# An attention layer with precise products: maxima from one-term scores, softmax sums taken after the exponentials, and a new order of the work

## Chip, cores and metric

The kernel runs on one core of one Trainium2 chip. The metric is the device time of one execution in microseconds (us). Engines are named as in the profile: PE (TensorE, matmuls), DVE (VectorE), ACT (ScalarE), POOL (GpSimd), SP (SyncE, here the queue that issues all transfers).

## What is computed

```python
h = _layernorm(x)                                   # x: 16 x 512 x 512
mod = jax.nn.silu(time) @ mod_w + mod_b
shift, scale, gate = jnp.split(mod, 3, axis=-1)
h = h * (scale + 1.0) + shift
qkv = (h @ w_qkv).reshape(B, T, 3, H, e)...         # 16 heads of 32
q = _apply_rope(_layernorm(q, q_norm_w), position)
k = _apply_rope(_layernorm(k, k_norm_w), position)
scores = jnp.einsum('bhqe,bhke->bhqk', q, k) / jnp.sqrt(e)
attn = jax.nn.softmax(scores, axis=-1)
o = jnp.einsum('bhqk,bhke->bhqe', attn, v)
return x + o @ w_out * gate
```

All is float32. The kernel gets its precision from splitting an operand into a rounded high part (type fp32r) and a low part (the rest), and adding three products of parts, "terms": high x high, high x low, low x high.

## The kernel before, in words

**Tiles and groups.** Each of the 16 batches has 512 rows, four tiles of 128: 64 tiles. The 16 heads of a batch make four groups of four heads: 64 groups. In step `s` (0 to 63) the attention of group `s` is done, and beside it the projections of tile `s + 6` (and later the output product of tile `s - 4`). A step has four quarters, one for each 128 rows. `FIRST` to -1 are the steps of the lead-in, without attention.

**A tile.** DVE takes the statistics (L605, L611), the inverse roots by eleven small instructions (`inverse_roots`, L633 to L642) and normalises (L650, L653). PE transposes the tile (`transpose_x`, L252), ACT writes the high part (`x_high`), DVE the low part (`x_low`, L665). PE makes q, k and v (`project`, L261, twelve matmuls each, into bank `Y`). ACT squares and moves q and k (L492, L493) and moves v (L504). DVE sums the squares (L616) and scales (`normalize_qk`, L660), and POOL rotates (`rotate`, L851, L856, L859, for q and for k).

**A group.** PE transposes q and k into the one bank `O` (`transpose_qk`, L352); DVE writes their parts (`qk_parts`, L674, L676). PE then makes the scores twice. By query (`scores_by_query`, L370, three terms of four matmuls in the four banks of `SM` and `MB`): DVE takes the row maxima (`maxima`, L683), ACT the exponentials with their row sums (`query_exponentials`, L527), ACT and DVE the shift `max + log(sum)` (`logarithm`, `log_sum_parts`, L690 to L696), which PE transposes (`transpose_c`, L379). By key (`scores_by_key`, L397, three terms, and L401, which adds the shift by a matmul against ones): ACT takes the exponentials, which are then final probabilities (`key_exponentials`, L542, L543), and PE weighs the values (`weigh_values`, L415, into `O`).

**Output.** ACT moves `O` (L519), DVE splits it (`output_parts`, L712, L714), PE multiplies with `w_out` (`project_out`, L268), DVE applies the gate (L705), POOL adds the residual (L864).

**Order.** Every engine runs its instructions in the order in which they are written, and waits are counts of semaphores. In quarter `q` of step `s`, PE does `scores_by_query(s + 1, q)`, a `weigh_values`, eight matmuls of a projection, `scores_by_key(s, q)` and the last four of the projection. `scores_by_key` waits for the exponentials by query in the same banks (L388).

Of the kernel before, what the change touches and what calls it, by code (L numbers as in the profile page):

```python
# [10 lines left out]
I32 = mybir.dt.int32  # L11

P = 128
RSQRT_MAGIC = 0x5F3759DF
NEWTON = 11


def cond_attention_kernel(nc, x, cond, position, mod_w, mod_b, w_qkv, w_out, q_norm_w, k_norm_w, out):
# [17 lines left out]
    FIRST = -8  # L36
# [12 lines left out]
    def early(s):  # L49
        return s < -1  # L50

    def v_tile(s):
        if s == -1:
            return -1
        return s + 6 if early(s) else s + 5

    with ExitStack() as ctx:
# [3 lines left out]
        def sem(name):  # L61
# [13 lines left out]
        xin = sb("xin", [P, 3, D])  # L75
# [6 lines left out]
        qk_hi = sb("qk_hi", [P, 3, 2, T], F32R)  # L82
        qk_lo = sb("qk_lo", [P, 3, 2, T], F32R)
        cst = sb("cst", [P, TT, P], F32R)
        cT = sb("cT", [P, T], F32R)
        probs = sb("probs", [P, 2, HG, T])
# [5 lines left out]
        negmax = sb("negmax", [P, 2, TT, HG])  # L92
        sums = sb("sums", [P, 2, TT, HG])
        lns = sb("lns", [P, TT, HG])
        row_shift = sb("row_shift", [P, TT, HG])
        bn = sb("bn", [P, 6])
# [3 lines left out]
        newton = sb("newton", [P, 1 + 2 * H])  # L100

# [7 lines left out]
        ld_modw, ld_modb, ld_wout = sem("ld_modw"), sem("ld_modb"), sem("ld_wout")  # L109
        ld_w = [sem("ld_wq"), sem("ld_wk"), sem("ld_wv")]  # L110
        ld_cond, ld_tables = sem("ld_cond"), sem("ld_tables")
        ld_x = [sem("ld_x0"), sem("ld_x1"), sem("ld_x2")]
        ld_res, st_y = sem("ld_res"), sem("st_y")
        ld_gate, ld_ss, ld_last, st_mod = sem("ld_gate"), sem("ld_ss"), sem("ld_last"), sem("st_mod")
# [3 lines left out]
        qkT_done, qm_done, cT_done, s_done, pv_step = (  # L118
            sem("qkT_done"), sem("qm_done"), sem("cT_done"), sem("s_done"), sem("pv_step"))
        siluT_done, mod_product = sem("siluT_done"), sem("mod_product")  # L120

        h_hi, squared, raw_out, v_out, o_out = (
            sem("h_hi"), sem("squared"), sem("raw_out"), sem("v_out"), sem("o_out"))
        qm_exp, ln_done, cT_out, s_exp = sem("qm_exp"), sem("ln_done"), sem("cT_out"), sem("s_exp")
        cond_exp, w_high, mod_out, wout_high = sem("cond_exp"), sem("w_high"), sem("mod_out"), sem("wout_high")
# [3 lines left out]
        x_scaled, h_lo, qk_high, qk_low, max_out, c_step, c_ready, y_gated = (  # L129
            sem("x_scaled"), sem("h_lo"), sem("qk_high"), sem("qk_low"), sem("max_out"), sem("c_step"),  # L130
            sem("c_ready"), sem("y_gated"))
        o_high, o_low, last_high, last_low, wout_low = (
            sem("o_high"), sem("o_low"), sem("last_high"), sem("last_low"), sem("wout_low"))
        ident_ready, silu_step, silu_ready, siluT_ready = (
            sem("ident_ready"), sem("silu_step"), sem("silu_ready"), sem("siluT_ready"))
        w_step, w_centred, w_low, table_step, tables_ready, stats_set, last_added = (
            sem("w_step"), sem("w_centred"), sem("w_low"), sem("table_step"), sem("tables_ready"),
            sem("stats_set"), sem("last_added"))

        consts, rope_step, res_added = sem("consts"), sem("rope_step"), sem("res_added")  # L140
# [3 lines left out]
        modw_raw = rows[:].rearrange("p a t j d -> p (a t j d)")[:, 4 * D:4 * D + DT * 3 * D].rearrange(  # L144
            "p (c n) -> p c n", c=DT)
        cond_sb = oT[0:NB, 0, 0, :]
        silu_sb = oT[0:NB, 0, 1, :]
        siluT = oT[:, 0, 2, 0:DT * NB].rearrange("p (c b) -> p c b", c=DT)
# [26 lines left out]
        def _(sp):  # L175
# [7 lines left out]
            for t in range(2):  # L183
                sp.dma_start(xin[:, t, :], x_t[0, t]).then_inc(ld_x[t], 16)
# [6 lines left out]
            def load_x(n):  # L191
                sp.wait_ge(xT_done, n - 2)
                sp.dma_start(xin[:, n % 3, :], x_t[n // TT, n % TT]).then_inc(ld_x[n % 3], 16)
# [704 lines left out]
```

## Time and profile before

| | |
|---|---|
| median of 3 runs | 1943.38 us (1943.3 to 1945.53) |
| profiled execution | 1946.49 us, span 1944.7 us |
| busy, share of the span | PE 91%, ACT 76%, DVE 76%, POOL 22% |
| lead-in, to the first `transpose_c` | 142.0 us |
| a step in the middle | 27.9 us |
| the last five steps | 160 us |

The table is read so: the middle, 59 steps, is 85% of the span. In it PE does nearly all the time something, while each other engine has gaps; ahead of it and behind it PE has gaps.

### The profile page before, as it was taken

What the parts mean: (1) busy time and instruction counts of PE and PEld (TensorE: products, weight loads), DVE (VectorE), ACT (ScalarE), POOL (GpSimd) and SP (SyncE); (2) the same over time, 40 slices, a digit from 0 to 9 for tenths busy, and PEclk for the clock granted to TensorE, in tenths of its full rate; (3) what the DMA queues carried; (4) which work ended last, traced back from release to release, by engine and by line L of the source; (5) the groups of instructions that cost most, each with busy time, mean ns of one, the idle gap of its engine ahead of it and who ended that gap; (6) DMA issues with size and microseconds to landing.
All of it is one profiled execution on the core that took longest, in us unless ns stands there. A gap on an engine that the chain in (4) does not pass through costs nothing.

```text
span 1944.7 us, 35999 instructions
## 1 busy us (share of the span) xinstructions
PE 1776.7 (91%) x13346; PEld 1030.4 (53%) x13346; DVE 1485.0 (76%) x2430; ACT 1487.2 (76%) x3145; POOL 434.4 (22%) x452
## 2 busy tenths in 40 slices
PE   4768899999999999999999999999999999997777
PEld 1645555555555555555555555555555555554333
DVE  6677778888888788878887888788878888875443
ACT  2248888888888888888888888888888888887663
POOL 0331222122212221222122212221222122221000
PEclk8879999999999999999999999999999999998769
DMA  5000010100101111010101010010111002000001
GB/s 193 27 6 28 6 44 23 50 28 17 55 28 50 34 39 34 23 55 17 55 28 50 23 49 29 18 55 28 50 33 40 28 17 63 16 28 22 21 18 66
DMA packets 35950, 72.77 MB, mean 37 GB/s; under 512 B 4513, under 2 KB 4513, under 8 KB 35778
## 3 DMA queue, kind: packets, MB, share of 16 engines
q1 hardware_dynamic: 35778, 70.47, 11.3%
q8 instruction: 109, 1.79, 0.4%
q14 instruction: 63, 0.52, 0.1%
HBM read 53.58 MB, written 16.88 MB: 36 GB/s over the span
## 4 chain that ended last, share of the span: by engine, by line
PE 80%; ACT 9%; issue 5%; DVE 5%; DMA 1%; ACTq 0%; SPq 0%; DVEq 0%
PE Y L261 26%; PE SM L370 13%; PE SA L397 10%; PE O L415 10%; PE Y L268 10%; ACT SM L527 4%; PE SA L401 3%; PE O L352 3%; PE SA L252 2%; ACT vals L504 2%; PE SA L379 2%; DVE qk_lo L676 1%; DVE qk_hi L674 1%; ACT probs L542 1%; ACT oT L519 1%
## 5 line engine op out<-in xcount | busy, mean ns | idle before, releaser
L527 ACT ACTIVATE SM<-SM,negmax 128x512 f32<-128x512 f32 x512 | 338.7, 664 | 130.8 <-DVE negmax L683 130.8
L683 DVE TENSOR_REDUCE negmax<-SM 128x2 f32<-128x1024 f32 x256 | 313.6, 1225 | 162.6 <-PE MB L370 155.9
L851 POOL TENSOR_TENSOR pair_part<-rows,rope_pair 128x256 f32<-128x256 f32 x128 | 94.5, 739 | 1312.8 <-DVE rows L660 1307.7
L527 ACT ACTIVATE MB<-MB,negmax 128x512 f32<-128x512 f32 x512 | 341.9, 671 | 0.0
L542 ACT ACTIVATE probs<-SM 128x1024 f32<-128x1024 f32 x256 | 262.8, 1027 | 72.0 <-PE SM L401 54.6
L683 DVE TENSOR_REDUCE negmax<-MB 128x2 f32<-128x1024 f32 x256 | 310.9, 1215 | 0.0
L261 PE MATMUL Y<-wqkv_hi,hT_hi 128*128 128x512 f32 x728 | 307.4, 422 | 0.3 <-ACT rows L493 0.3
L261 PE MATMUL Y<-wqkv_hi,hT_lo 128*128 128x512 f32 x728 | 306.7, 421 | 0.0
L415 PE MATMUL O<-probs,vals 128*32 128x512 f32 x2048 | 283.8, 627 | 5.9 <-ACT probs L543 5.9
L261 PE MATMUL Y<-wqkv_lo,hT_hi 128*128 128x512 f32 x728 | 289.2, 397 | 0.0
L543 ACT ACTIVATE probs<-SA 128x1024 f32<-128x1024 f32 x256 | 260.8, 1019 | 0.0
L261 PEld LDWEIGHTS Y<-wqkv_hi,hT_hi 128*128 128x128 f32 x728 | 139.1, 191 | 116.4 <-ACT rows L493 98.0
L674 DVE CAST qk_hi<-O 128x512 fp32r<-128x512 f32 x128 | 88.6, 692 | 146.0 <-PE O L352 146.0
L261 PEld LDWEIGHTS Y<-wqkv_hi,hT_lo 128*128 128x128 f32 x728 | 138.8, 191 | 67.6 <-issue 42.6
L370 PE MATMUL SM<-qk_hi 32*128 32x512 f32 x512 | 131.8, 499 | 45.2 <-ACT probs L542 18.6
L856 POOL TENSOR_TENSOR rows<-rows,rope_same 128x512 f32<-128x512 f32 x128 | 164.8, 1287 | 10.0
L397 PE MATMUL SA<-qk_hi 32*128 32x512 f32 x512 | 128.8, 496 | 38.5 <-ACT SM L527 37.8
L261 PEld LDWEIGHTS Y<-wqkv_lo,hT_hi 128*128 128x128 f32 x728 | 139.2, 191 | 24.3
L370 PEld LDWEIGHTS SM<-qk_hi 32*128 32x128 f32 x512 | 54.3, 187 | 147.9 <-issue 140.1
L370 PE MATMUL MB<-qk_hi 32*128 32x512 f32 x512 | 131.6, 510 | 0.0
L397 PE MATMUL SM<-qk_hi 32*128 32x512 f32 x512 | 129.9, 502 | 0.0
L510 ACT ACTIVATE cT<-SA 128x512 fp32r<-128x512 f32 x64 | 38.4, 600 | 109.9 <-PE SA L379 109.9
(140 smaller groups left out, 4108.6 us busy)
## 6 DMA issues: line engine op xcount, KB each, us to landing
xin<-in_x_dram SPq DMA_DIRECT2D x64, 256.0 KB, 2.9
xres<-in_x_dram SPq DMA_DIRECT2D x60, 256.0 KB, 2.6
out_dram<-xres SPq DMA_DIRECT2D x60, 256.0 KB, 2.0
shift_scale<-mod_rows SPq DMA_DIRECT2D x16, 512.0 KB, 4.2
gate<-mod_rows SPq DMA_DIRECT2D x16, 256.0 KB, 4.7
rows<-in_L_cond_mod_w_dram SPq DMA_DIRECT2D x1, 3072.0 KB, 10.0
probs<-in_L_cond_w_qkv_dram SPq DMA_DIRECT2D x2, 1024.0 KB, 12.7
vals<-in_L_cond_w_qkv_dram SPq DMA_DIRECT2D x1, 1024.0 KB, 15.6
```

What stands on the lines that cost most here:

```text
L261: mm = pe.matmul(bank, a[:, k, :], w[:, k, j * D:(j + 1) * D], start=(m == 0), stop=(m == 11))
L268: mm = pe.matmul(bank, o[:, g, :], w[:, g, :], start=(m == 0), stop=(m == 11))
L370: mm = pe.matmul(qm_bank(i), a[r, ring, 0, cols], c[r, ring, 1, :], start=(a is qk_hi and c is qk_hi), stop=(a is qk_lo))
L397: pe.matmul(s_bank(i), a[r, ring, 1, cols], c[r, ring, 0, :], start=(a is qk_hi and c is qk_hi), stop=False)
L415: mm = pe.matmul(O[head_rows(i), :], vals[:, b % 2, t, E * h:E * (h + 1)], probs[:, n % 2, i, :], start=(t == 0), stop=(t == TT - 1), skip ...
L527: ins = act.activation(qm_bank(i), qm_bank(i), ACT.Exp, bias=negmax[:, g % 2, t, i:i + 1], accum_out=sums[:, g % 2, t, i:i + 1])
L542: act.activation(probs[:, n % 2, 2:4, :], SM[:], ACT.Exp).then_inc(s_exp, 1)
L543: act.activation(probs[:, n % 2, 0:2, :], SA[:], ACT.Exp).then_inc(s_exp, 1)
L674: dve.tensor_copy(qk_hi[:, i, j, :], O[:]).then_inc(qk_high, 1)
L683: dve.tensor_reduce(negmax[:, g % 2, t, 2 * half:2 * half + 2], bank[:], AX.X, ALU.max, negate=True).then_inc(max_out, 1)
L851: pool.tensor_tensor(pair_part[:].rearrange("p h (i two) -> p h i two", two=2), swapped, rope_pair[:, t, j, :].rearrange("p (i two) -> p i ...
L856: pool.tensor_tensor(r, r, rope_same[:, t, j, :].unsqueeze(1).to_broadcast([P, H, E]), ALU.mult).then_inc(rope_step, 1)
```

## The change

- `scores_by_query` makes only the first term, high x high: four matmuls in place of twelve. From it come the maxima alone. `query_exponentials`, `logarithm` and `log_sum_parts` are gone; DVE writes the negated maxima straight into `cst`.
- The exponentials by key are thus not yet divided by their sum. The four probability blocks of a group (128 keys x 4 heads x 512 queries each, three buffers) are added: block 1 onto block 0 by POOL, block 2 by a transfer that POOL issues and that adds at its destination, block 3 by POOL (`add_keys`). PE sums over the 128 keys with ones (`add_over_keys`, into `MB`), ACT makes the inverse (`log_sums`, `inverse_sums`), DVE multiplies it onto the output (`scale_o`). The last group has two PE sums in place of the third addition.
- q and k are transposed into `MB`, both at once; ACT writes their high parts (`high_qk`), DVE the low parts (`low_qk`). Two buffers in place of three.
- `inverse_roots` has four instructions in place of eleven, and starts from a guess that ACT makes with Ln and Exp (`guess_roots`). ACT squares from `rows` behind the move.
- Step and quarters are reordered: a projection is twelve matmuls in one piece, v of tile `s + 4`, q and k of tile `s + 6`, the output product of tile `s - 5`. `output_parts` stands first in a step on DVE.
- The lead-in is written out by hand: weights in another order, modulation in three pieces (four matmuls at once in four column blocks, then one matmul that adds the blocks), its first row straight into `shift_scale`. POOL makes two of the low parts of the weights. Rotations wait for the third modulation piece (`mod_partial`).

```diff
+    def sum_buffer(g):
+        return 2 * (g % 2)
+    def probs_buffer(g, t):
+        return 1 if t % 2 else (sum_buffer(g) if t == 0 else 2 - sum_buffer(g))
...
             def scores_by_query(g, t):
...
+                if t == 1 and g >= 2:
+                    pe.wait_ge(sum_ln, g - 1)
                 if n > 0:
-                    pe.wait_ge(qm_exp, 2 * n)
...
+                    pe.wait_ge(max_out, 2 * n)
+                if g > 0:
+                    pe.wait_ge(s_exp, 2 * (n - TT) + 1)
...
-                for a, c in ((qk_hi, qk_hi), (qk_hi, qk_lo), (qk_lo, qk_hi)):
-                    for i in range(HG):
...
+                for i in range(HG):
+                    r = head_rows(i)
+                    mm = pe.matmul(qm_bank(i), qk_hi[r, g % 2, 0, cols], qk_hi[r, g % 2, 1, :], start=True, stop=True)
...
             def transpose_c(g):
-                pe.wait_ge(c_ready, g + 1)
+                pe.wait_ge(max_out, 2 * TT * (g + 1))
...
-                pe.wait_ge(qm_exp, 2 * (n + TT) + 1 if group(g + 1) else 2 * TT * NS)
...
+                if group(g + 1) or t == 0:
+                    pe.wait_ge(max_out, 2 * (n + TT - 1) + 1)
...
+            def add_over_keys(g, bank, buffers):
...
+                        mm = pe.matmul(bank[head_rows(i), :], ones_r[:, 0:E].bitcast(F32), probs[:, a, i, :],
...
+            modulation_parts(1, SM[:, 1, :])
+            modulation_parts(0, SM[:, 0, :])
...
+            project(3, 2, MB[:, 1, :])
+            modulation_parts(2, O[:])
...
+                    pe.wait_ge(third_added, s)
...
+                    add_over_keys(s - 1, MB[:, 0, :], (sum_buffer(s - 1),))
...
+            def high_qk(g, j):
+                act.wait_ge(qkT_done, 2 * g + j + 1)
...
+                act.activation(sum_inv[:], bank, ACT.Ln).then_inc(sum_ln, 1)
...
+                act.activation(sum_inv[:], sum_inv[:], ACT.Exp, scale=-1.0).then_inc(sum_ready, 1)
...
+                            act.wait_ge(second_added, 16 * g)
...
+                        act.wait_ge(third_added, g)
...
+                        act.wait_ge(first_added, g + 1)
...
-                for i in (2 * half, 2 * half + 1):
-                    ins = act.activation(qm_bank(i), qm_bank(i), ACT.Exp, bias=negmax[:, g % 2, t, i:i + 1],
-                                         accum_out=sums[:, g % 2, t, i:i + 1])
...
+            def scale_o(g):
+                o = oT[:, (g // NG) % 2, g % NG, :]
+                dve.wait_ge(sum_ready, g + 1)
+                dve.wait_ge(o_out, g + 1)
+                dve.tensor_tensor(o, o, sum_inv[:], ALU.mult).then_inc(o_scaled, 1)
...
+            def add_keys(g, t):
+                to = probs[:, sum_buffer(g)].rearrange("p h n -> p (h n)")
+                more = probs[:, probs_buffer(g, t)].rearrange("p h n -> p (h n)")
+                pool.wait_ge(s_exp, 2 * (TT * g + t) + 2)
+                if t == 1:
+                    pool.wait_ge(pv_step, TT * g + 1)
+                    pool.tensor_tensor(to, to, more, ALU.add).then_inc(first_added, 1)
+                elif t == 2:
+                    pool.wait_ge(first_added, g + 1)
+                    pool.dma_start(to, more, accum_op=ALU.add).then_inc(second_added, 16)
+                else:
+                    pool.wait_ge(second_added, 16 * (g + 1))
+                    pool.tensor_tensor(to, to, more, ALU.add).then_inc(third_added, 1)
...
+            pool.wait_ge(mod_partial, 3)
+            for n in range(5):
+                rotate(n, 0)
+                rotate(n, 1)
```

The order on POOL, a step in the middle. Before, a tile's rotation (L851, L856, L859, for q and for k) and a residual (L864):

```order
L864 TENSOR_TENSOR xres<-xres,gated 128x512
L851 TENSOR_TENSOR pair_part<-rows,rope_pair 128x256
L856 TENSOR_TENSOR rows<-rows,rope_same 128x512
L859 TENSOR_TENSOR rows<-rows,pair_part 128x16x16
L851 TENSOR_TENSOR pair_part<-rows,rope_pair 128x256
L856 TENSOR_TENSOR rows<-rows,rope_same 128x512
L859 TENSOR_TENSOR rows<-rows,pair_part 128x16x16
```

And in the changed kernel (L1176 and L1182 are the additions of block 1 and block 3, L1179 the adding transfer):

```order
L1176 TENSOR_TENSOR probs<-probs 128x2048
L1179 DMA probs<-probs 128x2048
L1153 TENSOR_TENSOR pair_part<-rows,rope_pair 128x256
L1158 TENSOR_TENSOR rows<-rows,rope_same 128x512
L1161 TENSOR_TENSOR rows<-rows,pair_part 128x16x16
L1153 TENSOR_TENSOR pair_part<-rows,rope_pair 128x256
L1158 TENSOR_TENSOR rows<-rows,rope_same 128x512
L1161 TENSOR_TENSOR rows<-rows,pair_part 128x16x16
L1182 TENSOR_TENSOR probs<-probs 128x2048
L1166 TENSOR_TENSOR xres<-xres,gated 128x512
```

Three instructions were added, and the rotation now stands between the issue of the transfer and the addition that waits for it.

The order on DVE around the start of a step. Before, from the maxima of the last quarter (`negmax`) to the split of the output:

```order
L683 TENSOR_REDUCE negmax<-SM 128x2
L683 TENSOR_REDUCE negmax<-MB 128x2
L674 CAST qk_hi<-O 128x512
L676 TENSOR_TENSOR qk_lo<-O,qk_hi 128x512
L674 CAST qk_hi<-O 128x512
L676 TENSOR_TENSOR qk_lo<-O,qk_hi 128x512
L683 TENSOR_REDUCE negmax<-SM 128x2
L683 TENSOR_REDUCE negmax<-MB 128x2
L616 TENSOR_REDUCE stats<-squares 128x16
L605 BN_STATS bn<-xin 128x6
L712 CAST o_hi<-oT 128x512
L714 TENSOR_TENSOR o_lo<-oT,o_hi 128x512
```

And now (L938 maxima, L960 and L962 the split of the output):

```order
L945 TENSOR_TENSOR oT<-oT,sum_inv 128x512
L905 SCALAR_TENSOR_TENSOR xin<-xin,stats,shift_scale 128x512
L908 SCALAR_TENSOR_TENSOR xin<-xin,rstd,shift_scale 128x512
L860 BN_STATS bn<-xin 128x6
L866 BN_AGGR stats<-bn 128x2
L938 TENSOR_REDUCE cst<-SM 128x2
L938 TENSOR_REDUCE cst<-MB 128x2
L872 TENSOR_REDUCE stats<-squares 128x16
L960 CAST o_hi<-oT 128x512
L962 TENSOR_TENSOR o_lo<-oT,o_hi 128x512
L927 TENSOR_TENSOR qk_lo<-MB,qk_hi 128x512 x2
```

The split of the output moved ahead of the low parts of q and k, and three instructions with two operands in SBUF (L945, L905, L908) stand ahead of the last maxima.

## Rows read from the trace of the kernel before

**Rows 1.** Windows by stage: time, each engine busy (x instructions), granted clock, DMA share

```profile
100.00:142.00 42.00, 24.05 (x133) 16.55 (x131) 32.22 (x56) 17.19 (x44) 13.66 (x14) 0.77 0.01 2
170.00:1785.00 1615.00, 1547.48 (x12020) 900.79 (x12012) 1303.32 (x2115) 1332.92 (x2837) 389.74 (x402) 1.00 0.11 34
1785.00:1907.00 122.00, 91.80 (x651) 43.61 (x649) 54.58 (x69) 80.38 (x172) 4.53 (x4) 0.71 0.07 20
```

**Rows 2.** Timeline of PE: start us, us, operation; the end of a quarter

```profile
932.82 0.50 PE L261 MATMUL Y<-wqkv_hi,hT_lo 128*128 128x512 f32 x1
933.16 0.40 PE L261 MATMUL Y<-wqkv_hi,hT_hi 128*128 128x512 f32 x1
933.39 0.39 PE L261 MATMUL Y<-wqkv_lo,hT_hi 128*128 128x512 f32 x1
...
934.12 0.49 PE L370 MATMUL SM<-qk_hi 32*128 32x512 f32 x2
...
935.03 1.06 PE L415 MATMUL O<-probs,vals 128*32 128x512 f32 x8
936.02 0.50 PE L261 MATMUL Y<-wqkv_hi,hT_hi 128*128 128x512 f32 x1
```

**Rows 3.** Timeline of PE, `transpose_c` of two early steps, without output product

```profile
198.76 0.54 PE L379 MATMUL SA<-ident_r,cst 128*128 128x128 f32 x4
```

```profile
226.00 0.54 PE L379 MATMUL SA<-ident_r,cst 128*128 128x128 f32 x4
```

**Rows 4.** Chain in the middle, start us, us, what: two `transpose_c` in a row

```profile
921.83 0.47 PE SA L379 x4
...
949.72 0.47 PE SA L379 x4
```

**Rows 5.** Groups of instructions: count, busy us, mean ns, idle before

```profile
L527 ACT ACTIVATE SM<-SM,negmax 128x512 f32<-128x512 f32 x512 | 338.7, 664 | 130.8 <-DVE negmax L683 130.8
L683 DVE TENSOR_REDUCE negmax<-SM 128x2 f32<-128x1024 f32 x256 | 313.6, 1225 | 162.6 <-PE MB L370 155.9
```

**Rows 6.** Timelines of DVE and POOL at one moment: who holds up whom

```profile
945.67 0.74 POOL L851 TENSOR_TENSOR pair_part<-rows,rope_pair 128x256 f32<-128x256 f32 x1 [20.66 <-DVE rows L660]
946.49 1.29 POOL L856 TENSOR_TENSOR rows<-rows,rope_same 128x512 f32<-128x512 f32 x1
...
951.61 1.27 POOL L864 TENSOR_TENSOR xres<-xres,gated 128x512 f32<-128x512 f32 x1
```

```profile
946.55 1.27 DVE L694 CAST cst<-row_shift 128x16 fp32r<-128x16 f32 x1
...
947.96 0.69 DVE L705 TENSOR_TENSOR gated<-Y,gate 128x512 f32<-128x512 f32 x1
```

**Rows 7.** The same cast with POOL idle, and a POOL add beside a long DVE subtract

```profile
1842.21 0.18 DVE L694 CAST cst<-row_shift 128x16 fp32r<-128x16 f32 x1
```

```profile
100.52 2.30 DVE L790 TENSOR_TENSOR wout_lo<-oT,wout_hi 128x2048 fp32r<-128x2048 f32 x1 [1.12 <-ACT wout_hi L567]
```

```profile
100.75 2.67 POOL L859 TENSOR_TENSOR rows<-rows,pair_part 128x256 f32<-128x256 f32 x1
```

**Rows 8.** DMA issues: KB each, median us from issue to landing

```profile
xin<-in_x_dram SPq DMA_DIRECT2D x64, 256.0 KB, 2.9
...
rows<-in_L_cond_mod_w_dram SPq DMA_DIRECT2D x1, 3072.0 KB, 10.0
...
vals<-in_L_cond_w_qkv_dram SPq DMA_DIRECT2D x1, 1024.0 KB, 15.6
oT<-in_L_cond_w_out_dram SPq DMA_DIRECT2D x1, 1024.0 KB, 12.0
```

**Rows 9.** Chain of the last steps, one quarter: start us, us, what

```profile
1789.12 1.03 ACT probs L542
...
1791.99 1.24 DVE negmax L683
...
1796.97 1.03 ACT probs L542
```

More of the change, by code:

```diff
@@ L231, in _ @@
                     load_residual(s - 4)
+                if tile(s + 8) and (s + 8) % TT == 0:
+                    load_shift_scale((s + 8) // TT)
+            store(NT - 5)
             sp.wait_ge(qkT_done, 2 * NS)
@@ L464, in _ @@
+            pe.wait_ge(last_low, 3)
+            for t in range(3):
+                project_last(t, 2, 3)
+            weigh_values(LAST, 3)
+            pe.wait_ge(second_added, 16 * NS)
+            add_over_keys(LAST, SM[:, 0, :], (sum_buffer(LAST), probs_buffer(LAST, 3)))
+            project_last(3, 0, 3)
             pe.wait_ge(last_low, NG)
             for t in range(TT):
-                project_last(t, last_banks[t], 3, 4)
+                project_last(t, 3, 4)
         @block.scalar
@@ L585, in _ @@
+            log_sums(LAST, SM[:, 0, :])
+            inverse_sums(LAST)
         @block.vector
@@ new lines, in _ @@
+            x_statistics(6)
+            aggregate_x(6)
+            low_qk(0, 0)
+            low_qk(0, 1)
+            square_sums(4, 1)
+            maxima(0, 0)
+            x_low(5)
+            inverse_roots(6)
+            maxima(0, 1)
+            normalize_qk(4)
+            maxima(0, 2)
+            normalize_x(6)
+            maxima(0, 3)
+            x_statistics(7)
+            aggregate_x(7)
+            square_sums(5, 0)
+            for s in range(LAST + 1):
+                if s - 5 >= 0:
+                    output_parts(s - 5)
+                if group(s + 1):
+                    low_qk(s + 1, 0)
+                    low_qk(s + 1, 1)
+                    maxima(s + 1, 0)
+                if tile(s + 5):
+                    square_sums(s + 5, 1)
+                if group(s + 1):
+                    maxima(s + 1, 1)
+                if tile(s + 6):
+                    x_low(s + 6)
+                if s - 5 >= 0:
+                    apply_gate(s - 5, Y[:], gated[:])
+                if tile(s + 5):
+                    inverse_roots(s + 7)
+                    normalize_qk(s + 5)
+                if group(s + 1):
+                    maxima(s + 1, 2)
+                if s == LAST:
+                    output_parts(s - 4)
+                if s > 0:
+                    scale_o(s - 1)
+                if s == 1:
+                    dve.wait_ge(wout_high, 1)
+                    dve.tensor_tensor(wout_lo[:], wout_raw, wout_hi[:].bitcast(F32), ALU.subtract
+                                      ).then_inc(wout_low, 1)
+                if tile(s + 7):
+                    normalize_x(s + 7)
+                if tile(s + 8):
+                    x_statistics(s + 8)
+                    aggregate_x(s + 8)
+                if group(s + 1):
+                    maxima(s + 1, 3)
+                if tile(s + 6):
+                    square_sums(s + 6, 0)
+                if s == LAST:
+                    last_parts(0)
+                    last_parts(1)
+                    last_parts(2)
+                    apply_gate(s - 4, Y[:], gated[:])
```

1023 lines of the change are left out of this document (600 added, 423 removed).

## The prediction

> **What bounds the kernel now.** I read the windows by stage first. In the middle PE is busy 1547.5 of 1615 us at full granted clock, ACT and DVE some 1300 to 1330, POOL 390 [rows 1]. So PE is the first bound there, with the others close. The two ends are not at PE's bound: in the 42 us ahead of the first `transpose_c` PE is busy 24, and in the last steps 92 of 122 at a granted clock of 0.71. Then the timeline of PE, by starts, since matmuls overlap: a full matmul follows the last after 0.23 us, the first after a switch of shape after 0.34; three terms by query take from 934.12 to 935.03, 0.91 us; a `weigh_values` 0.99 [rows 2]. A step in the middle is 27.9 us from one `transpose_c` to the next [rows 4]. Early steps, which have no output product (3 us of PE), still take 27.24 us [rows 3]: PE is not alone, the loop of maxima and exponentials by query is as long. Both must shrink for a gain, and both do here.
>
> **The floor of the new step on PE.** Per step, by starts: four `scores_by_key` of 1.13 are 4.5; five sums over keys and values (four `weigh_values`, one `add_over_keys` of the same shape) of 0.99 are 5.0; four `scores_by_query` of one term, 0.91 less two terms of 0.23, are 1.8; three projections of twelve in one piece, 0.34 + 11 x 0.23 + 0.1 for leaving, are 8.9; the output product 3.0; transposes 1.9. Sum 25.1. Before, the same count gives 27.0 and the step 27.9. So PE's own work falls by 1.9 and another 0.9 of waits can go.
>
> **The other engines.** ACT loses sixteen exponentials by query, 0.66 us each [rows 5], 10.6 a step, and gains some six moves and small ones of 0.5 to 0.6, so it has much slack. DVE loses two casts, seven small ones and the shift, and gains `scale_o`; before it is busy 1303 us in 57.9 steps [rows 1], 22.5 a step, now by count 19 to 20, of it four pairs of maxima at some 2.3 [rows 5]. POOL gains two additions of 128x2048. From 0.74 us for 256 and 1.29 for 512 elements [rows 6], 2.15 ns an element, one is 4.6 us. POOL then has 9.3 + 5.9 (rotation) + 1.3 (residual) + the issue of the transfer, which no row shows; I take 1 us, between 0.3 and 2. That is 17.6, under 25.
>
> **By hand through one step**, zero at `transpose_c(s)`. Scores by key end at 2.5, first exponentials at 3.6, `low_qk` can end at 3.2, so `scores_by_query` starts at 3.7 (0.2 of wait). v to 7.1; key scores; `add_over_keys` at 8.2, which needs the third addition of the group before; output product and transpose to 14.25; then two quarters of 5.8 with 0.2 wait each for the SM half of the exponentials. End 25.8. The maxima of the last quarter would be done before `transpose_c` by 0.4. So waits that are in sight cost 0.7: **25.8**.
>
> **What POOL's long instructions do to DVE.** The trace shows the price. A cast of 16 elements takes 0.18 us with POOL idle and 1.27 beside a POOL multiplication that ends at 947.78; DVE's gate product, which reads PSUM, runs beside POOL at its 0.69 [rows 6, 7]. The other way round, POOL's add of 0.74 took 2.67 beside a DVE subtract of two SBUF operands and ended 0.6 after it [rows 7]. So the one that comes later stands still until the other's instruction ends. The page SBUF — State Buffer of the Trainium skill, section Who interferes with whom, says this of a DVE instruction with two SBUF inputs or a two-port mode against one of GpSimd that reads SBUF; by that rule, the trace agrees.
> Where do they meet in the new order? (a) Inverse roots at 15.1 against the first addition, 11.0 to 15.6: 0.5, hidden. (b) `scale_o` and the two normalisations, from 20.0, against the rotation, from 18.5 (exponentials of quarter 2 end at 17.5, issue 1 us). Each can wait for a rest of 0.6 to 1.3. With all three waits the last maxima end 1.7 late, and `transpose_c` with them; with none, 0. I take half, 0.8: a step of **26.6**. (c) The split of the output at about 0.6 to 1.7 of the step, against the third addition. That depends on when the addition starts, so on the transfer.
>
> **The transfer.** 1 MB within SBUF with addition is in no row. Between 256 KB in 2.9 us and 3072 KB in 10.0 [rows 8] 1 MB takes 4.8; since it reads both operands, 7.3 if reads count double. The row of the same size, 1024 KB of 128 x 2048, took 12.0, behind other loads. I take 11, nearest to the row of that size; the ends are 4.8 and 15.6, the longest landing of a load of that size [rows 8]. Issued at 17.5 it lands at 28.5, 1.9 into the next step: the split of the output is past, the exponentials of quarter 0 wait for it only from 2.6, and the third addition ends at 6.5, before 8.2. Then it costs nothing. The page DMA: Bandwidth & Descriptors of the Trainium skill, section Anatomy of one DMA, gives a fixed 2 us and bytes / 436e3 for a transfer issued by GpSimd, an estimate of 4.4 us here; by it the third addition starts as soon as the rotation ends, and the time would be that of the first rival below. No run here shows it yet.
>
> **Lead-in.** Before: 142.0, where the window of rows 1 ends. The modulation came first, then its round trip through memory, then each tile in one chain with eleven small instructions. Now: 3 MB of weights have landed at about 12, by 10.0 for 3072 KB [rows 8]; modulation pieces and the two additions to about 20, normalisation, first projection at about 24, twelve projections of 3.0 (some at half clock) to about 63. Rotations wait for the third modulation piece, so they run from 64, and group 0 needs four of 5.9 [rows 6]: 88. Then three projections, four maxima: first `transpose_c` at **107**, between 92 and 125.
>
> **Tail.** A quarter was 7.85 [rows 9]: exponentials, scores, maxima, exponentials by query, scores. Without the exponentials by query it is about 5.2 at half clock and 4.2 at full. With the output product and the sum in one quarter a step of 19 to 29; I take 23 in place of 30.5 (122 us for four, [rows 1]). The last step was some 37, from 1907 to the end at 1944.7; it loses exponentials but gains the wait for the last transfer, two sums, Ln, Exp and the scaling: 43.
>
> **Sum.** 107 + 5 early steps of 25.7 (128.5) + 53 steps of 26.6 (1410) + 2 with v alone of 22 (44) + 3 x 23 (69) + 43 = 1801.5 of span. Before, 1.8 us lie outside the span, and the median is 3.1 under the profiled run: **1800**. Against 1943.4 that is 7.4% less: 35 from the lead-in, 75 from the middle, the rest from the tail and the steps with no q and k.
>
> **Rivals.**
> *The split of the output is caught by the third addition; slower.* If the transfer lands within about 9 us, the third addition starts when the rotation ends, about 1 before the next step, and holds the port to 3.6. The cast stands until then, the residual add may slip in between cast and subtract (1.3), `low_qk` comes at 5 to 6 in place of 1.9, and `scores_by_query`, with the projection queued behind it on PE, starts 2.3 to 3.6 late. A step is 29.5 to 30.8, the whole 53 x 3.0 to 53 x 4.2 more: 1960 to 2025. It becomes slower than before from a step of 29.3. For it: the interpolated 4.8 to 7.3. Against it: no row shows a POOL instruction of over 1.3 us holding DVE, and with a landing like that of the 1024 KB loads, 12.0 or more, the addition comes after the split. Chance 0.13.
> *No meeting costs anything.* DVE's instructions fall in gaps, the step is 25.8 or a little under, the lead-in 95: 1745. Chance 0.22.
> *The transfer is late*, 13 to 15.6: quarter 0's exponentials wait, each us over 11.7 costs one a step, 58 in all: 1870 to 1980. Chance 0.13, a third of it slower than before.
> *The forecast's own case*, 1765 to 1850, chance 0.50. Two hundredths are left for surprises of the tail.
>
> **How the numbers follow.** The range of 8 in 10 takes the forecast's case, most of the case without meetings and the better half of the late transfer: 1735 to 1915. About 0.2% is what a measurement of this kernel can tell from no change. Faster: 0.50 + 0.22 + 0.08 + 0.02 + 0.01 of the first rival = 0.83; same 0.02; slower 0.15.
>
> **What would show it.** The distance between two `transpose_c` in the middle: 26.6, with PE waiting for the last maxima by under 1.7. In DVE's timeline the cast of the split at its 0.41 and not at 3 to 5; on POOL two adds of 4.6 a step; the landing of the adding transfer 10 to 12 after issue; the first `transpose_c` near 107. The prediction is wrong if the cast stretches, if exponentials of quarter 0 wait for the transfer, or if PE's granted clock in the middle is under 1.00.

## The result and the profile after

The changed kernel takes 2079.49 us (2070.99 to 2087.37, 4 runs) where the kernel before took 1943.34 beside it: the ratio is 1.0697, interval 1.0643 to 1.0752. It is slower by 7%, where 7.4% faster was forecast. Its profiled execution, the slowest of the four, took 2087.37, with a span of 2085.6. The forecast made the span up from six stages, of which the two steps with v alone and the three behind them are taken together here as the tail; measured by the starts of the copy of `cT` (L647), which follows each `transpose_c`, they are:

| stage | forecast us | measured us | miss us |
|---|---|---|---|
| lead-in, to the first `transpose_c` | 107 | 115.6 | +8.6 |
| 5 early steps | 128.5 | 142.2 | +13.7 |
| 53 steps | 1410 (26.6 each) | 1650.5 (31.1 each, median 30.8) | +240.5 |
| 5 steps of the tail | 113 | 134.0 | +21.0 |
| last step | 43 | 43.2 | +0.2 |

So 240 of the 284 us lie in the middle. The page of the changed kernel, against [rows 1, 5, 8]: busy time of the engines, the chain that ended last by engine and by line, three groups (busy us and mean ns of one after the bar, then idle before), and the new transfer's landing.

```profile
PE 1739.2 (83%) x11822; PEld 1030.8 (49%) x11822; DVE 1588.6 (76%) x1714; ACT 959.8 (46%) x1420; POOL 1143.7 (55%) x648
...
DVE 42%; PE 42%; issue 13%; ACT 1%; POOL 1%; DMA 1%; SPq 0%; DVEq 0%; POOLq 0%; ACTq 0%
...
L1176 POOL TENSOR_TENSOR probs<-probs 128x2048 f32<-128x2048 f32 x64 | 294.4, 4601 | 658.1 <-ACT probs L706 648.5
...
L1182 POOL TENSOR_TENSOR probs<-probs 128x2048 f32<-128x2048 f32 x63 | 287.5, 4564 | 38.6 <-DMA probs<-probs 38.6
...
L960 DVE CAST o_hi<-oT 128x512 fp32r<-128x512 f32 x60 | 199.5, 3325 | 0.0
...
probs<-probs POOLq DMA_DIRECT2D x64, 1024.0 KB, 7.0
```

More than half of the chain is not PE's. The line to stop at is L960: a cast of 128x512, which takes 0.42 us where nothing is in its way (below), has a mean of 3325 ns. The additions took the 4.6 us that were worked out for them, and the transfer landed after 7.0 on the median (6.9 to 9.2), not 11. Windows of the middle of the changed kernel (columns as in rows 1), which answer to the second row of [rows 1]:

```profile
258.00:1910.00 1652.00, 1417.10 (x9775) 846.19 (x9773) 1312.68 (x1373) 784.95 (x1169) 948.12 (x530) 0.94 0.27 65
```

PE is busy 86% of the stretch, in place of 96%, and its granted clock is 0.94 in place of 1.00. One step shows why. Timelines of POOL, of DVE and of PE, from one `transpose_c` (1000.46) on; the next step follows after 30.86:

```profile
998.58 0.74 POOL L1161 TENSOR_TENSOR rows<-rows,pair_part 128x256 f32<-128x256 f32 x1
999.28 4.56 POOL L1182 TENSOR_TENSOR probs<-probs 128x2048 f32<-128x2048 f32 x1
1003.80 1.44 POOL L1166 TENSOR_TENSOR xres<-xres,gated 128x512 f32<-128x512 f32 x1
```

```profile
1000.91 3.21 DVE L960 CAST o_hi<-oT 128x512 fp32r<-128x512 f32 x1
1004.16 1.64 DVE L962 TENSOR_TENSOR o_lo<-oT,o_hi 128x512 fp32r<-128x512 f32 x1
1005.72 1.28 DVE L927 TENSOR_TENSOR qk_lo<-MB,qk_hi 128x512 fp32r<-128x512 f32 x2
```

```profile
1000.46 0.54 PE L370 MATMUL SA<-ident_r,cst 128*128 128x128 f32 x4 [0.74 <-DVE cst L938]
...
1002.96 1.06 PE L411 MATMUL O<-probs,vals 128*32 128x512 f32 x8
1007.05 0.50 PE L362 MATMUL SM<-qk_hi 32*128 32x512 f32 x2 [3.03 <-DVE qk_lo L927]
...
1007.49 1.42 PE L308 MATMUL Y<-wqkv_hi,hT_hi 128*128 128x512 f32 x4
1008.71 1.91 PE L311 MATMUL Y<-wqkv_hi,hT_lo 128*128 128x512 f32 x4
1010.41 1.68 PE L315 MATMUL Y<-wqkv_lo,hT_hi 128*128 128x512 f32 x4
```

The third addition of the sums (block 3, by POOL) starts as the last rotation ends, 1.2 ahead of `transpose_c`, and ends at 1003.84. The cast stands from 1000.91 to 1004.12. POOL's residual addition then runs beside the subtract, which takes 1.64. The low parts of q and k come at 5.3 to 6.5 of the step, and PE, which has nothing else in its order, waits 3.03. Then it runs the projection of v, twelve matmuls, in 4.5 us instead of 3.0. The windows of those pieces give the clock:

```profile
1000.46:1007.40 6.94, 3.90 (x40) 2.25 (x40) 6.50 (x5) 4.52 (x7) 4.79 (x2) 1.00 0.10 38
1007.40:1012.02 4.62, 4.62 (x16) 3.31 (x12) 2.95 (x3) 0.00 (x0) 0.00 (x0) 0.63 0.49 170
1012.02:1031.32 19.30, 18.14 (x133) 10.42 (x132) 15.14 (x19) 10.27 (x15) 13.12 (x9) 1.00 0.32 69
```

After the stall the granted clock is 0.63, a mean over a piece spent mostly at 1.2 GHz; before and behind it is 2.4. So a step is the floor of 25.1, plus 3.0 of stall, 1.5 of clock, 0.7 of waiting for the last maxima (the first row of PE above) and 0.5 of the small waits by hand: 30.8.

In 13 of the 53 steps the transfer landed later than the rotation ended, and the addition started 0.7 to 1.5 later than in the others. That made it worse, not better: the cast was held for 4.0 to 4.7 us in place of 3.2, and those steps took 31.6 to 33.7.

### The profile page after: what moved, and what is told of

It reads as the page before. It is cut to its first block, busy times and chain, and to the rows that moved or that the text cites. A ratio compares the mean times of both kernels' runs of the same rounds, so it can differ in the third digit from the quotient of the medians.

```text
span 2085.6 us, 31004 instructions
## 1 busy us (share of the span) xinstructions
PE 1739.2 (83%) x11822; PEld 1030.8 (49%) x11822; DVE 1588.6 (76%) x1714; ACT 959.8 (46%) x1420; POOL 1143.7 (55%) x648
## 4 chain that ended last, share of the span: by engine, by line
DVE 42%; PE 42%; issue 13%; ACT 1%; POOL 1%; DMA 1%; SPq 0%; DVEq 0%; POOLq 0%; ACTq 0%
DVE cst L938 11%; DVE o_hi L960 9%; PE Y L321 8%; PE Y L308 6%; PE Y L311 5%; PE SA L392 4%; PE Y L315 4%; PE SM L362 4%; DVE oT L945 3%; DVE qk_lo L927 3%; PE O L411 3%; DVE xin L905 3%; PE MB L420 3%; DVE half_var L884 3%; DVE rows L915 2%
## 5 line engine op out<-in xcount | busy, mean ns | idle before, releaser
L1176 POOL TENSOR_TENSOR probs<-probs 128x2048 f32<-128x2048 f32 x64 | 294.4, 4601 | 658.1 <-ACT probs L706 648.5
L938 DVE TENSOR_REDUCE cst<-SM 128x2 fp32r<-128x1024 f32 x256 | 311.8, 1218 | 382.7 <-PE MB L362 382.7
L362 PE MATMUL SM<-qk_hi 32*128 32x512 f32 x512 | 139.6, 534 | 210.6 <-DVE qk_lo L927 177.2
L938 DVE TENSOR_REDUCE cst<-MB 128x2 fp32r<-128x1024 f32 x256 | 311.5, 1217 | 0.0
L1182 POOL TENSOR_TENSOR probs<-probs 128x2048 f32<-128x2048 f32 x63 | 287.5, 4564 | 38.6 <-DMA probs<-probs 38.6
L308 PE MATMUL Y<-wqkv_hi,hT_hi 128*128 128x512 f32 x724 | 254.6, 480 | 1.7 <-ACT hT_hi L590 1.7
L311 PE MATMUL Y<-wqkv_hi,hT_lo 128*128 128x512 f32 x724 | 229.3, 445 | 2.4 <-DVE hT_lo L921 2.4
L621 ACT ACTIVATE rows<-Y 128x512 f32<-128x512 f32 x123 | 73.5, 597 | 306.4 <-PE Y L315 306.4
L315 PE MATMUL Y<-wqkv_lo,hT_hi 128*128 128x512 f32 x724 | 211.9, 419 | 0.0
L641 ACT ACTIVATE vals<-Y 128x512 f32<-128x512 f32 x61 | 36.5, 598 | 360.7 <-PE Y L315 360.7
L960 DVE CAST o_hi<-oT 128x512 fp32r<-128x512 f32 x60 | 199.5, 3325 | 0.0
## 6 DMA issues: line engine op xcount, KB each, us to landing
probs<-in_L_cond_w_qkv_dram SPq DMA_DIRECT2D x2, 1024.0 KB, 11.2
```

The lines of the kernel that those rows point to most:

```text
L308: pe.matmul(bank, x_hi[:, k, :], wqkv_hi[:, k, cols], start=(k == 0), stop=False)
L311: pe.matmul(bank, x_lo[:, k, :], wqkv_hi[:, k, cols], start=False, stop=False)
L315: mm = pe.matmul(bank, x_hi[:, k, :], wqkv_lo[:, k, cols], start=False, stop=(k == DT - 1))
L362: mm = pe.matmul(qm_bank(i), qk_hi[r, g % 2, 0, cols], qk_hi[r, g % 2, 1, :], start=True, stop=True)
L938: dve.tensor_reduce(heads[:, 2 * half:2 * half + 2, 0], bank[:], AX.X, ALU.max, negate=True).then_inc(max_out, 1)
L960: dve.tensor_copy(o_hi[:], oT[:, b % 2, :, cols]).then_inc(o_high, 1)
```

## Experiments

Each theory's numbers stand in the expectations. Step means the time from one `cT` copy to the next in the middle, the median where nothing else is said. Experiments 1, 5 and 7 were timed three or four times, the others once. Five runs of the kernel before beside them lie within 0.2% of each other and the four of the changed kernel within 0.8%, so differences of some 50 us are read, and ones of 3 us are not.

### 1. The split of the output behind the first maxima

```
                if group(s + 1):
                    low_qk(s + 1, 0)
                    low_qk(s + 1, 1)
                    maxima(s + 1, 0)
+               if s - 5 >= 0:
+                   output_parts(s - 5)
```

(and the pair of lines that calls `output_parts` ahead of `low_qk` gone). 

> The changed kernel with one edit: DVE's split of the output (cast L960 and subtract L962) stands behind the maxima of quarter 0, not ahead of the low parts of q and k. Port theory (the third addition on POOL holds the split, 2.8 us, the residual add the subtract, 0.95, and PE stands 3.0 us and then runs 1.5 us longer at half clock): the split now falls where POOL idles, cast 0.41 us, the step falls from 30.8 to 26.0 to 27.4 us, the whole to 1830 to 1910. Rival, the load theory (the step is long because DVE, POOL and PE together have too much to do, so that work moved only moves the wait): 30 us or more a step, 2040 to 2090.

Measured: 1824.35 us, ratio to the kernel before 0.9382 (0.9361 to 0.9403); step 26.5. One move of two instructions on DVE turns 7% slower into 6% faster. The middle and, on DVE, the split and `scale_o`:

```profile
258.00:1650.00 1392.00, 1317.02 (x9699) 779.82 (x9697) 1099.83 (x1367) 779.76 (x1161) 931.88 (x524) 1.00 0.31 77
```

```profile
L945 DVE TENSOR_TENSOR oT<-oT,sum_inv 128x512 f32<-128x512 f32 x63 | 82.0, 1301 | 0.0
...
L960 DVE CAST o_hi<-oT 128x512 fp32r<-128x512 f32 x60 | 26.7, 444 | 0.0
```

The cast is back at 444 ns and the clock at 1.00, while all additions and the transfer are still there. A step lost 4.4 us by the meeting (30.84 to 26.45); stall and clock had been counted at 4.5. The step lies in the range of the port theory, the whole 6 us under it.

### 2. The third addition behind the split

```
                     pool.wait_ge(second_added, 16 * (g + 1))
+                    if g >= 4:
+                        pool.wait_ge(o_low, g - 3)
```

> The changed kernel with one more wait on POOL and nothing moved on DVE: the third addition waits for the split of the output of the next step (o_low). Port theory: the addition starts 1.7 us into the step in place of 1.1 ahead of it, ends at 6.3, ahead of the 8.2 at which PE needs it; the step falls to 26.6 to 27.4 as with the late split, the whole to 1850 to 1910. Load theory: a wait more on POOL can only cost, 31 us or more a step.

Measured: 1820.94 us, step 26.4. Here DVE's order is the changed kernel's own, and only POOL is told to wait. The group of the third addition:

```profile
L1184 POOL TENSOR_TENSOR probs<-probs 128x2048 f32<-128x2048 f32 x63 | 289.2, 4591 | 184.7 <-DVE o_lo L962 178.5
```

A wait of 178.5 us in sum on POOL, 2.8 a step, gains 259 us of time. The cause is the moment of the meeting, not DVE's order. The step is 0.2 and the whole 29 under the lower ends of the port theory.

### 3. The additions cut to 16 columns

```
-                    pool.tensor_tensor(to, to, more, ALU.add)
+                    pool.tensor_tensor(to[:, 0:16], to[:, 0:16], more[:, 0:16], ALU.add)
```

(both additions; the sums leave out most columns, and the logarithm gets a small bias.) 

> The changed kernel with POOL's two additions cut to the first 16 of 2048 columns (the softmax sums are then incomplete; the transfer, all waits and all other work stay; the logarithm gets a small bias). It measures what the two additions cost in all. Port theory: with them gone only the rotation and the residual meet DVE: 25.8 to 26.6 us a step, 1800 to 1850. Load theory: POOL's 9.2 us a step were not on the path, since POOL idles a third of the time: 29 us or more a step.

Measured: 1825.31 us, step 26.5. The first addition, and DVE's half variance and `scale_o`, in this kernel:

```profile
L1176 POOL TENSOR_TENSOR probs<-probs 128x16 f32<-128x16 f32 x64 | 14.3, 224 | 688.9 <-ACT probs L706 688.9
```

```profile
L945 DVE TENSOR_TENSOR oT<-oT,sum_inv 128x512 f32<-128x512 f32 x63 | 105.4, 1674 | 0.0
...
L884 DVE TENSOR_SCALAR half_var<-stats 128x33 f32<-128x33 f32 x64 | 11.1, 173 | 0.3
```

With 553 us less work on POOL than in experiment 1 (581.8 us busy against 1134.9) the step is that of experiments 1 and 2. Both numbers are in the port theory's range. So 9 us of additions a step cost nothing but the meeting with the split. (The meeting (a) of the forecast, of the half variance with the first addition, is seen to go: 173 ns against 996 in experiment 1; nothing came of it, as was said.) `scale_o`, which stands beside the rotation, is still held: there is the rest of the loss.

### 4. A transfer that lands late

```
                     pool.dma_start(to, more, accum_op=ALU.add).then_inc(second_added, 16)
+                    pool.dma_start(spare, wqkv_hi[:, :, 0:D]).then_inc(spare_out, 16)
...
                     pool.wait_ge(second_added, 16 * (g + 1))
+                    pool.wait_ge(spare_out, 16 * (g + 1))
```

> The changed kernel with a second transfer of 1 MB (weights to a spare place in memory, used by nothing) issued by POOL behind the adding one, and the third addition waits for both. It gives the third addition the late start that the prediction had assumed (11 us after issue in place of 7.0). Port theory: if both have landed 11 to 13 us after the issue, the split passes ahead of the addition and the step falls to 27 to 28 us, the whole to 1880 to 1940, faster with more transfers. If it costs POOL a second issue of 0.9 us and DVE meets a later rotation, up to 29. Load theory: 31 us or more.

Measured: 1828.33 us, step 26.4. The third addition and the landings of the two transfers:

```profile
L1186 POOL TENSOR_TENSOR probs<-probs 128x2048 f32<-128x2048 f32 x63 | 295.6, 4693 | 161.3 <-DMA spare<-wqkv_hi 157.1
...
probs<-probs POOLq DMA_DIRECT2D x64, 1024.0 KB, 7.1
spare<-wqkv_hi POOLq DMA_DIRECT2D x64, 1024.0 KB, 9.8
```

This is the forecast's case made true: 1 MB of traffic more a step, and the kernel is 251 us faster than the changed one, since the addition starts 0.9 to 2.9 behind `transpose_c` (median 1.6) and no longer 1.2 ahead of it, and the cast, which starts 0.45 behind it, gets past. The experiment's own ranges, 27 to 28 a step and 1880 to 1940 in all, were too high; the forecast of 26.6 a step holds where the transfer is as late as it assumed.

### 5. `scale_o` moved too

The pair ahead of `low_qk` is gone as in experiment 1, and `scale_o` is for the group one step earlier.

```
                     maxima(s + 1, 0)
+                if s > 1:
+                    scale_o(s - 2)
+                if s - 5 >= 0:
+                    output_parts(s - 5)
...
-                if s > 0:
+                if s == LAST:
                     scale_o(s - 1)
```

> Nothing is left out of the computation. Edit on the changed kernel: output_parts(s-5) and scale_o both stand behind maxima(s+1,0) on VectorE, scale_o for the group before the last (s-2), so nothing that reads two SBUF operands stands between the rotation of GpSimd and maxima(s+1,3) but the two normalisations. In the kernel that moved the split alone a step is 26.5, of it 0.7 a wait of the transposition of the maxima for the last maxima. Meeting theory: scale_o stood behind the rotation there; without it the last maxima come at least 0.7 earlier, that wait goes and a step is 25.7 to 26.0: 1780 to 1800 in all. Rival theory: the normalisations hold VectorE as before, and the multiplication, now near the second long addition, only moves the loss: 26.3 to 26.7, 1815 to 1835.

Measured: 1773.02 us (1771.82 to 1775.86), ratio 0.9118 (0.9103 to 0.9133); step 25.5, in all 53 steps. That is 0.2 and some 7 us under the lower ends of the meeting theory. Windows of the middle, and DVE beside POOL's first addition, which runs from 1004.86 to 1009.49:

```profile
258.00:1600.00 1342.00, 1306.50 (x9676) 782.68 (x9676) 1074.37 (x1367) 772.31 (x1158) 914.79 (x525) 1.00 0.33 80
```

```profile
1006.83 0.68 DVE L921 TENSOR_TENSOR hT_lo<-SA,hT_hi 128x512 fp32r<-128x512 f32 x1
1007.95 0.69 DVE L953 TENSOR_TENSOR gated<-Y,gate 128x512 f32<-128x512 f32 x1 [0.44 <-PE Y L321]
1008.56 0.97 DVE L884 TENSOR_SCALAR half_var<-stats 128x33 f32<-128x33 f32 x1
```

```profile
1004.86 4.63 POOL L1178 TENSOR_TENSOR probs<-probs 128x2048 f32<-128x2048 f32 x1 [4.62 <-ACT probs L706]
```

PE is busy 97% of the middle and waits nowhere but 0.2 for the exponentials in three quarters of four: this is the by-hand step without a meeting that costs (25.8), three tenths shorter. The rival, that the loss would only move, falls, though the two normalisations still meet the rotation. The rows also show which of these instructions of DVE ran beside a long addition: the two that read PSUM take their 0.68 and 0.69, while the half variance, which reads and writes SBUF alone, ends when the addition ends.

### 6. The projection of v ahead of the stall

```
                 if tile(s + 4):
                     ...
                     project(s + 4, 2, Y[:])
+                if group(s + 1):
+                    scores_by_query(s + 1, 0)
```

(in the changed kernel, on TensorE; the pair of lines ahead of it gone.) 

> Nothing is left out. Edit on the changed kernel: in quarter 0 on TensorE the projection of v stands ahead of scores_by_query(s+1,0), in place of behind it; VectorE and GpSimd are as in the changed kernel, so the cast is still held 3.2 us. A step is 30.8 there. If the hold costs only because TensorE has nothing to do until the low parts come, the 3.0 of the projection fills the gap at full clock: the stall falls from 3.0 to under 0.5 ahead of the query scores, the 1.5 us that the projection took longer at half clock go too, and a wait for the first maxima of about 1 comes in ahead of scores_by_key(s,1): a step of 27.7 to 28.5, 1900 to 1945 in all, with a granted clock of 0.98 or more in the middle. If the low clock has another cause than the stall, the clock in the middle stays at 0.94 and a step is 29.2 to 30: 1980 to 2030.

Measured: 1957.72 us, mean step 28.6, granted clock 0.98. Most steps take 27.8; 21 of 53 take 29.5 or more, each with a stretch at 1.2 GHz in it, and in 11 steps PE still waits 0.6 to 1.6 for the low parts. The time lies past the upper end of the first theory (28.5 a step, 1945) and well under the other's (29.2, 1980). The waits of PE from 300 to 1500, and the windows of quarter 1 in a long and in a short step (the sum over keys, values and the output product):

```profile
PE SA L392 <- DVE cst L938: 58.5, 41, 1.4
PE SA L370 <- DVE cst L938: 32.5, 42, 0.8
...
PE SM L362 <- DVE qk_lo L927: 8.2, 8, 1.6
```

```profile
1013.42:1021.96 8.54, 8.54 (x53) 4.13 (x53) 4.53 (x5) 4.09 (x7) 3.60 (x1) 0.80 0.11 34
...
1043.00:1049.85 6.85, 6.85 (x56) 3.96 (x56) 4.50 (x5) 4.09 (x7) 3.03 (x1) 1.00 0.15 43
```

The cast is held as long as before (3.2, same order), but the stall of 3.0 is filled; in its place comes a wait of 1.4 for the first maxima. 25.5 + 1.4 + 0.8 for the last maxima is 27.7, which is the short step. So most of the loss comes from PE having nothing to do at that moment, and the low clock goes with the stall in 32 of 53 steps, where the changed kernel had it in every one. In the long steps it comes back, right behind the wait of 1.4: quarter 1 takes 8.54 with PE busy throughout, at a clock of 0.80, where the short step takes 6.85. The wait ahead of it is the same 1.4 in both. Why the clock falls behind one of them and not behind the other stays open.

### 7. The third modulation piece early

```
             project(1, 1, MB[:, 0, :])
+            modulation_parts(2, O[:])
             pe.wait_ge(v_out, 1)
...
             project(3, 2, MB[:, 1, :])
-            modulation_parts(2, O[:])
```

(on the kernel of experiment 5.) 

> Nothing is left out. The kernel with both moves, and the eight matmuls of the third modulation piece on TensorE after project(1,1), near 47 us, in place of after project(3,2), near 64. Theory: in the changed kernel GpSimd idles 32.3 us until that piece, then rotates four tiles back to back until 89.7, and the first cT copy is at 115.6. With the piece early each rotation follows its normalisation (the last at 64.8), so they end near 71 to 73 and the first cT copy comes at 97 to 102: 14 to 18 us less than the same kernel without it, about 1765 to 1785 in all. Rival: rotations beside the normalisations hold VectorE, the projections of the lead-in wait and half is lost: first copy at 104 to 110, 6 to 11 us less.

Measured: 1759.78 us (1758.06 to 1761.23), ratio 0.9047 (0.9033 to 0.9060): the fastest of all. The first `cT` copy is at 102.5 in place of 115.6, between the two expectations. POOL's first rotation in the changed kernel, then the first and the last for group 0 here, and what then took time on PE:

```profile
64.96 1.10 POOL L1153 TENSOR_TENSOR pair_part<-rows,rope_pair 128x256 f32<-128x256 f32 x1 [32.26 <-PE O L435]
```

```profile
47.52 0.74 POOL L1155 TENSOR_TENSOR pair_part<-rows,rope_pair 128x256 f32<-128x256 f32 x1 [14.81 <-DVE rows L915]
...
76.29 0.73 POOL L1163 TENSOR_TENSOR rows<-rows,pair_part 128x256 f32<-128x256 f32 x1
```

```profile
73.30 2.08 PE L311 MATMUL Y<-wqkv_hi,hT_lo 128*128 128x512 f32 x4 [4.37 <-DVE hT_lo L921]
```

The gain of 13 us is 1 short of the theory's 14, and the whole 5 under its 1765. The rotations end at 77.0, not at 71 to 73, since the last normalisation now stands behind small instructions of DVE that rotations hold (0.74, 1.23 and 0.78 us for ones of 0.18 to 0.20), and the projection of tile 4 waits for DVE's queue. The theory is right in the main, 13 us, and the rival's mechanism is seen at work for the rest.

### 8. Three terms by query, with the split late

```
-                for i in range(HG):
+                for a, c in ((qk_hi, qk_hi), (qk_hi, qk_lo), (qk_lo, qk_hi)):
+                    for i in range(HG):
...
```

(on the kernel of experiment 1.) 

> Nothing is left out. The kernel with the split late (1824.35, step 26.5), with scores_by_query in three terms in place of one, as in the kernel before: two terms more cost TensorE 0.46 for each of four tiles, 1.8 a step. If TensorE's own work now bounds the step, it is 28.0 to 28.4 and the whole 1910 to 1940. If VectorE's chain of maxima bounds it, half or less shows: 26.8 to 27.5, 1845 to 1885.

Measured: 1886.28 us, step 27.4, 0.95 over experiment 1. By the expectation's words the step (26.8 to 27.5) speaks for the chain of maxima as the bound (the whole is 1 us over that theory's 1885). Its window says something finer:

```profile
300.00:1700.00 1400.00, 1365.07 (x11045) 823.25 (x11047) 1048.02 (x1328) 750.32 (x1124) 906.37 (x510) 1.00 0.31 75
```

PE is busy 97.5% and no wait for the last maxima is left. 25.5, the step with PE as the bound (experiment 5), plus the 1.84 of two terms in four tiles (0.23 each) is 27.3. So with one term the bound was the chain of the last maxima with `scale_o` held in it, at 26.5, and with three it is PE. By these numbers one term is worth 1.9 a step when the meetings are gone too and 0.95 when they are not; three terms in the order of experiment 5 were not run.

### 9 and 10. What the transfer costs

```
-                    pool.dma_start(to, more, accum_op=ALU.add).then_inc(second_added, 16)
+                    pool.dma_start(to, more).then_inc(second_added, 16)
```

> Edit on the kernel with both moves (1773.02 us): the transfer of 1 MB within SBUF copies in place of adding, so the sums leave out two of four parts (the logarithm gets a bias so that it stays finite). It measures what the addition in the transfer costs. If the price is the bytes moved, operands read twice (the 7.3 of the forecast's working), a copy lands in 4.6 to 5.2 us after its issue in place of 7.0. If the addition is free and the price lies in the packets, it stays at 6.5 to 7.0. The total tells nothing here: GpSimd rotates until after the landing in both, 1768 to 1778.

```
+                    pool.dma_start(to[:, 0:1024], more[:, 0:1024], accum_op=ALU.add).then_inc(second_added, 16)
```

> Edit on the kernel with both moves: the adding transfer takes 1024 of the 2048 columns, 512 KB, so the sums leave out part of one tile (the logarithm gets a bias so that it stays finite). If the price is a fixed part of some 2 us and the rest goes by bytes, it lands in 4.3 to 4.8 us; if it is set by the number of rows and packets and not by bytes, in 6 to 7. The total stays at 1768 to 1778.

The landings, of the copy and of the half, beside 7.0 for the whole addition:

```profile
probs<-probs POOLq DMA_DIRECT2D x64, 1024.0 KB, 4.6
```

```profile
probs<-probs POOLq DMA_DIRECT2D x64, 512.0 KB, 4.5
```

Both are as expected of a price by bytes. From 7.0 and 4.5 an adding transfer costs 2.0 us and 5.0 per MB, if it goes by a fixed part and bytes; if the copy has the same 2.0, it costs 2.6 per MB, and the addition about doubles the part that goes by bytes. The copy was taken at one size only, so its fixed part is assumed. The totals, 1773.37 and 1776.12, are within 3.1 of experiment 5: in that order the landing does not matter. The page DMA: Bandwidth & Descriptors of the Trainium skill, section Anatomy of one DMA, gives 2 us and bytes / 436e3, an estimate of 4.4 for 1 MB; the copy agrees with it at 4.6, the adding transfer, at 7.0, does not.

## Why the prediction was wrong

**The step that failed is the choice of 11 us for the transfer.** With it the third addition was put behind the split of the output, and the meeting (c) at nothing. The forecast had worked out 4.8 from the rows of other sizes, and 7.3 "if reads count double"; then it took 11, "nearest to the row of that size". The chip gave 4.6 for a copy and 7.0 for the adding one: both worked numbers were right within 0.3. The rows of 12.0 and 15.6 [rows 8] are loads of the start, in flight with megabytes of others. Windows of the kernel before while they ran (columns as in rows 1, with GB/s last):

```profile
15.00:20.00 5.00, 5.00 (x10) 0.86 (x9) 3.81 (x14) 0.59 (x1) 0.00 (x0) 1.00 1.05 399
20.00:25.00 5.00, 5.00 (x12) 0.89 (x11) 4.93 (x4) 0.59 (x1) 0.00 (x0) 1.00 1.05 387
```

All sixteen DMA engines are busy the whole time, so these rows hold the delay of other loads and say little of what a transfer costs by itself. Size was the wrong likeness; what else is in flight was the right one.

**A threshold made this step decisive.** The forecast said itself that a landing within about 9 us brings the third addition ahead of the next `transpose_c`, and the first rival priced what follows: a step of 29.5 to 30.8, 1960 to 2025 in all. Measured is 30.8. Up to the stall the mechanism is the rival's to the letter: the addition starts 1.2 ahead of the step (it said 1), holds to 3.4 (3.6), the residual addition slips in between cast and subtract (1.64 for the subtract), the low parts come at 5.3 to 6.5 (5 to 6), PE waits 3.03 (2.3 to 3.6). Its chance of 0.13 was the same error again, since it rested on the price of 11. "No row shows a POOL instruction of over 1.3 us holding DVE" was weak evidence: in the trace of before only one POOL instruction is longer than 1.4 us, the 2.67 of rows 7, and that one was itself held. The page SBUF — State Buffer of the Trainium skill, section Who interferes with whom, gives the shared ports to whichever instruction comes first, for the whole of it. By that rule, the trace agrees: the cast took 3.2 us, until the 4.56 of the addition were over.

**What the rival left out.** It reached 30.8 with a start of the projection up to 3.6 late and 0.6 more that it does not account for; measured are 3.0 of stall and 1.5 of low clock behind it, which is in no term. That its 30.8 is met is in part luck. That a stall costs clock too could be read in [rows 1], where the tail ran at 0.71. The time of 2087 lies past the rival's upper end of 2025: 18 us because the mean step is 31.1 and not 30.8 (the 13 late landings above, 11.2 us of waiting in sum), and 44 at the ends (8.6, 13.7 and 21.0 in the table).

**What held.** PE's floor of 25.1 and the by-hand 25.8: measured 25.5 in experiment 5. The forecast of 26.6 with meeting (b) and without (c): 26.4 to 26.5 in experiments 1, 2 and 4. The price of meeting (b) taken as 0.8: 1.0 between experiments 1 and 5, of it 0.8 as the wait for the last maxima. The additions at 4.6 us (4564 and 4601 ns), the issue at 1 us (0.88), the last step at 43 (43.2). The tail holds in part: without the meeting its five steps take 121.4 and 121.6 in experiments 1 and 5, against 113 forecast, and 134.0 with it. In experiment 1 the last three take 23.7 each on the mean (23 forecast), but the two with v alone take 25.1 each (22 forecast).

**Lead-in and early steps** were taken too short by 22 together in the changed kernel. The rotations ended at 89.7, near the 88 of the forecast, but the four maxima behind them took 26 us rather than 19. The windows of the changed kernel from that moment, and two of PE's waits there:

```profile
90.54:115.62 25.08, 15.69 (x64) 10.38 (x63) 15.47 (x21) 4.47 (x10) 6.27 (x6) 0.77 0.04 11
```

```profile
99.83 1.66 PE L311 MATMUL Y<-wqkv_hi,hT_lo 128*128 128x512 f32 x4 [1.84 <-DVE hT_lo L921]
...
110.71 0.80 PE L362 MATMUL SM<-qk_hi 32*128 32x512 f32 x2 [2.89 <-DVE cst L938]
```

PE and DVE wait for each other in turn, tile by tile, at a clock of 0.77; the estimate had counted instructions and no such turns. The five early steps have the same look: 142.2 at a clock of 0.91 in the changed kernel, still 139.5 in experiment 5, of them 30.7 for the first alone. They have no split of the output, so the meeting with it is not their cause. Which wait sets them was not tried.

By the sum: with the rival's 30.8 a step and the measured ends the span is 2067, 18 short of the measured 2085.6. With the transfer as late as was assumed, 1828.33 (experiment 4) against a forecast of 1800 is a miss of 1.6%: the ends were taken 35 us too short and the middle 10 too long.

Three slips in the working bear on nothing above. The line through the rows of 256 and 3072 KB gives 7.4, not 7.3, with reads counted double. POOL's terms add up to 17.5, not 17.6. By its own rule of one us a step for each us over 11.7, a landing at 15.6 gives about 2025, not 1980, at the upper end of the late transfer.

## What to carry over

When two engines exclude each other, an instruction's place in time is part of its cost: ask of each long GpSimd instruction when its trigger fires at the earliest, not only at the likeliest, and look what VectorE issues in that window with SBUF operands alone. If a short instruction stands there ahead of work that TensorE waits for, put it behind that work, even if nothing forces it at the expected times; here this is worth 12%, and a transfer that landed sooner than forecast was the harmful one. When a forecast rests on a threshold, give the price that crosses it a chance of its own from every row that bears on it, above all from the rows that hold no queue.

## What was not expected of the hardware

- A VectorE cast of 0.42 us took 3.2 us beside one GpSimd instruction (3325 ns on the mean of 60); maxima, which read PSUM, keep their 1217 ns beside the additions.
- A gap of 3 us on TensorE was followed by some 4.6 at a granted clock of 0.63, in which twelve matmuls took 4.5 us in place of 3.0. With the gap filled by the same projection a step was 2.5 us shorter on the mean, though VectorE was held as long (experiment 6).
- A transfer within SBUF that adds takes 7.0 us for 1 MB, a copy 4.6, an adding one of half the size 4.5.
- More work made the kernel faster: a second transfer of 1 MB a step, or a wait of 2.8 us on GpSimd, gained 251 and 259 us.
